# Decoder layer on one core: the output projection's weight scale, half by maximum on VectorE and half by row sums of squares on ScalarE

## What is computed

```
ctx = ctx.transpose(0, 2, 1, 3).reshape(N, S, N_HEADS * D_HEAD)
return ctx @ Wo + bo
...
x = x + _L0_attn_ref(_layernorm(x, axis=-1), Wq, Wk, Wv, Wo, bo)
```

## Time and profile before

| | us |
|---|---|
| median of 3 runs | 1280.59 |
| the three runs | 1277.7, 1280.98, 1280.59 |
| the profiled execution, whole time | 1277.78 |
| its span, first to last instruction | 1276.0 |
| PE busy | 1214.5 (95%) |
| DVE busy | 941.7 (74%) |
| ACT busy | 603.6 (47%) |
| POOL busy | 567.5 (44%) |
| mean granted TensorE clock | 0.989 |

### The profile page before, as it was taken

How to read it: one execution, slowest core, us unless ns; L and a number is a source line. 1 busy time by engine, 2 the same in 40 slices (tenths; PEclk the granted TensorE clock), 3 DMA queues, 4 the chain that set the end, 5 groups by cost and what they waited for, 6 DMA issues and landing times.

```text
span 1276.0 us, 20047 instructions
## 1 busy us (share of the span) xinstructions
PE 1214.5 (95%) x7263; PEld 828.6 (65%) x7278; DVE 941.7 (74%) x1283; ACT 603.6 (47%) x718; POOL 567.5 (44%) x491
## 2 busy tenths in 40 slices
PE   4977999999999999999999879999799999999998
PEld 3644555657557566575565457777587877877784
DVE  5799778877887788788887968888736545554654
ACT  5685584674765847747658610000134323432331
POOL 1444253543634535435355429999433222322321
PEclk9999999999999999999999989999899999999999
DMA  9462323542435235434355346775000000000000
GB/s 307 131 204 89 110 69 112 153 152 86 132 127 152 83 104 154 148 92 126 111 160 171 127 97 131 148 136 126 1 1 1 18 18 3 15 16 17 1 18 33
DMA packets 128006, 123.77 MB, mean 97 GB/s; under 512 B 31628, under 2 KB 89234, under 8 KB 127954
## 3 DMA queue, kind: packets, MB, share of 16 engines
q1 hardware_dynamic: 103000, 116.86, 30.5%
q10 hardware_dynamic: 24960, 6.29, 3.4%
HBM read 81.63 MB, written 35.21 MB: 92 GB/s over the span
## 4 chain that ended last, share of the span: by engine, by line
PE 80%; ACT 6%; DVE 6%; issue 5%; POOL 2%; DMA 1%; SPq 0%; ACTq 0%; DVEq 0%; POOLq 0%
PE bank L815 12%; PE bank L581 9%; PE bank L582 9%; PE bank L583 9%; PE bank L863 9%; PE bank L864 9%; PE bank L666 6%; PE bank L886 4%; PE bank L885 4%; PE bank L667 3%; PE bank L645 3%; PE bank L644 3%; ACT region_c L984 2%; POOL parts L1755 1%; ACT rsum L955 1%
## 5 line engine op out<-in xcount | busy, mean ns | idle before, releaser
L863 PE MATMUL bank<-h_hi,guT 128*128 128x256 f16 x1024 | 226.3, 274 | 1.4 <-DVE h_lo L1643 1.4
L864 PE MATMUL bank<-h_lo,guT 128*128 128x256 f16 x1024 | 226.2, 274 | 0.0
L1755 POOL TENSOR_TENSOR parts<-parts 128x512 f32<-128x512 f32 x80 | 130.6, 1636 | 180.8 <-DVE parts L1238 180.5
L581 PE MATMUL bank<-hT_hi,w_hi 128*128 128x256 f16 x640 | 175.9, 275 | 0.5 <-DVE hT_lo L1223 0.5
L582 PE MATMUL bank<-hT_lo,w_hi 128*128 128x256 f16 x640 | 175.8, 275 | 0.0
L583 PE MATMUL bank<-hT_hi,w_lo 128*128 128x256 f16 x640 | 175.7, 275 | 0.0
L815 PE MATMUL bank<-kv,toep 128*128 128x288 f32 x640 | 159.4, 413 | 5.4 <-POOL kv L1797 2.9
L1760 POOL TENSOR_SCALAR_AFFINE_SELECT region_c<-region_c 128x512 f32<-128x512 f32 x128 | 103.2, 830 | 120.8 <-ACT region_c L987 120.8
L815 PEld LDWEIGHTS bank<-kv,toep 128*128 128x128 f32 x640 | 123.4, 193 | 40.9 <-DVE prod L1606 3.3
L666 PE MATMUL bank<-region_c,v 128*128 128x512 f32 x256 | 133.3, 602 | 13.3 <-DVE ctx L1259 13.1
L984 ACT ACTIVATE region_c<-bank,cap_scale 128x1536 f32<-128x1536 f32 x64 | 98.7, 1542 | 52.8 <-PE bank L645 52.5
(11 more groups left out here) (161 smaller groups left out, 2512.6 us busy)
## 6 DMA issues: line engine op xcount, KB each, us to landing
unit_halves<-halves SPq DMA_DIRECT2D x80, 256.0 KB, 2.3
q_both<-unit_halves SPq DMA_DIRECT2D x64, 256.0 KB, 3.0
wffn<-w_gu SPq DMA_DIRECT2D x8, 1024.0 KB, 5.5
q_high<-unit_halves SPq DMA_DIRECT2D x64, 128.0 KB, 3.1
toep<-kernel_padded SPq DMA_DIRECT2D x32, 256.0 KB, 4.0
cpair<-ctx_pairs SPq DMA_DIRECT2D x32, 176.0 KB, 4.8
xin<-x SPq DMA_DIRECT2D x8, 512.0 KB, 3.5
region_o<-wq SPq DMA_DIRECT2D x4, 1024.0 KB, 12.1
```

What stands on the lines that cost most here:

```text
L581: pe.matmul(dst, lh, rh, start=first and k == 0, stop=False)
L863: pe.matmul(dst, guT[:, k, col:col + P], h3_hi[:, p, k, :], start=(k == 0), stop=False)
L864: mm = pe.matmul(dst, guT[:, k, col:col + P], h3_lo[:, p, k, :], start=False, stop=(k == DB - 1))
L1755: pool.tensor_tensor(slot[:, 0], slot[:, 0], slot[:, 1], ALU.add).then_inc(unit_summed, 1)
```

## The change

Wo's size is found in two ways. Pieces 0, 1, 3 and 5 still go by maximum on DVE, one at the end of each of the steps 4 to 7. Pieces 2, 4, 6 and 7 go by row sums of squares on ACT (`sum_wo_rows`, one in step 5, one in step 6, two in step 7); their by-product goes to `wo_hi[0]`. In step 8 DVE squares the four maxima, takes the larger of maxima and row sums, reduces over four and lays the diagonal (`largest_row_of_wo`). `find_scale` then takes the square root's exponent for weight 6 too, by the same number of steps.

SP issues four pieces (2 to 5) after unit 7's load back, and 6 and 7 after unit 8's. ACT's row sums of Q3 move behind the values' high part. PE's `top(I_O)` is written at step 9 ahead of `values`, which is the same place in PE's order. ACT's `high_wo(0)` and `(1)` move ahead of `high_unit(1, 2)`. `lay_bias(0)` waits for the key bias alone, and `bo` is waited for at the first `output`.

```
         BY_ROWS = range(I_K + 1, I_O)
+        WO_BY_MAX, WO_BY_ROWS = (0, 1, 3, 5), (2, 4, 6, 7)
...
-            sp.dma_start(key_bias_s[bias_rows], key_bias).then_inc(consts_in, 16)
+            sp.dma_start(key_bias_s[bias_rows], key_bias).then_inc(key_bias_in, 16)
...
-            sp.dma_start(bo_s[:], bo.partition_broadcast(P)).then_inc(consts_in, 16)
+            sp.dma_start(bo_s[:], bo.partition_broadcast(P)).then_inc(bo_in, 16)
...
-                if n == UNITS - 1:
+                if n == 8:
                     sp.wait_ge(w_rounded, 1)
-                for c in range(2 * (n - 6), 2 * (n - 5)) if n >= 6 else ():
+                for c in {6: (0, 1), 7: (2, 3, 4, 5), 8: (6, 7)}.get(n, ()):
                     sp.dma_start(wo_raw[c], wo.rearrange("(k p) n -> p k n", p=P)[:, o_rows[c], :]).then_inc(wo_in[c], 16)
...
+                    if step == NG + 1:
+                        pe.wait_ge(tanh_done, NG)
+                        top(I_O)
                     values(0, step - 2, True)
...
-                    if step == NG:
-                        pe.wait_ge(tanh_done, NG)
-                        top(I_O)
...
+            def sum_wo_rows(c):
+                act.wait_ge(wo_in[c], 16)
+                n = WO_BY_ROWS.index(c)
+                if n:
+                    act.wait_ge(wo_row_summed, n)
+                act.activation(wo_hi[0], wo_raw[c], ACT.Square, accum_out=wmax_row[:, n:n + 1]).then_inc(wo_row_summed, 1)
...
                 high_unit(0, 0, True)
-                sum_rows(I_Q[3])
                 high_unit(0, 1, True)
                 high_weight(I_V)
+                sum_rows(I_Q[3])
                 high_unit(0, 2, True)
...
+                    if step == NG + 1:
+                        for c in range(O_SHIFT):
+                            high_wo(c)
                     if 7 <= step < 7 + len(AHEAD_BANKS):
                         high_unit(1, step - 7)
...
-                    if step == NG + 1:
-                        for c in range(O_SHIFT):
-                            high_wo(c)
+                    for c in {5: (2,), 6: (4,), 7: (6, 7)}.get(step, ()):
+                        sum_wo_rows(c)
...
-                if n in BY_ROWS:
+                if n != I_K:
...
                 if c == 0:
-                    dve.wait_ge(consts_in, 16 * N_CONST)
+                    dve.wait_ge(key_bias_in, 16)
...
-                if c == O_PIECES - 1:
-                    dve.wait_ge(wpiece_done, O_PIECES)
-                    dve.tensor_reduce(wmax[:, I_O:I_O + 1], wmax_piece[:], AX_X, ALU.max).then_inc(wmax_done, 1)
-                    square(I_O)
+            def largest_row_of_wo():
+                dve.wait_ge(wpiece_done, len(WO_BY_MAX))
+                dve.tensor_tensor(wmax_piece[:], wmax_piece[:], wmax_piece[:], ALU.mult).then_inc(wpiece_done, 1)
+                dve.wait_ge(wo_row_summed, len(WO_BY_ROWS))
+                dve.wait_ge(wpiece_done, len(WO_BY_MAX) + 1)
+                dve.tensor_tensor(wmax_piece[:], wmax_piece[:], wmax_row[:], ALU.max).then_inc(wpiece_done, 1)
+                dve.wait_ge(wpiece_done, len(WO_BY_MAX) + 2)
+                dve.tensor_reduce(wmax[:, I_O:I_O + 1], wmax_piece[:], AX_X, ALU.max).then_inc(wmax_done, 1)
+                square(I_O)
...
+                    if step == NG:
+                        largest_row_of_wo()
                     normalise(0, step - 2, True)
...
-                    for c in {4: (0, 1), 5: (2, 3), 6: (4, 5), 7: (6, 7)}.get(step, ()):
+                    for c in {4: (0,), 5: (1,), 6: (3,), 7: (5,)}.get(step, ()):
                         largest_of_wo(c)
...
                     if n == EARLY - 1:
+                        dve.wait_ge(bo_in, 16)
                         for i in range(TT):
                             output(0, i)
```

More of the change, by code:

```diff
@@ L152, in decoder_layer @@
             wmax = sb1("wmax", [P, SCALES])
-            wmax_piece = sb1("wmax_piece", [P, O_PIECES])
+            wmax_piece = sb1("wmax_piece", [P, O_PIECES // 2])
+            wmax_row = sb1("wmax_row", [P, O_PIECES // 2])
             wtop = sb1("wtop", [P, SCALES])
@@ L245, in decoder_layer @@
         BY_ROWS = range(I_K + 1, I_O)
+        WO_BY_MAX, WO_BY_ROWS = (0, 1, 3, 5), (2, 4, 6, 7)
         def square_and_ones(n):
             return (early_squares[:, n], early_squares[:, SCALES]) if n != I_O else (wo_square, wo_ones)
-        consts_in = sem("consts_in")
+        key_bias_in = sem("key_bias_in")
+        bo_in = sem("bo_in")
         ident_in = sem("ident_in")
@@ L260, in decoder_layer @@
         wpiece_done = sem("wpiece_done")
+        wo_row_summed = sem("wo_row_summed")
         wmax_done = sem("wmax_done")
@@ L353, in decoder_layer @@
         out_stored = sem("out_stored")
-        N_ROPE, N_CONST = 2, 2
+        N_ROPE = 2
         QUANT_STORES = 16 * (1 + WQT - GUT)
@@ L1327, in largest_of_wo @@
             def largest_of_wo(c):
+                n = WO_BY_MAX.index(c)
                 dve.wait_ge(wo_in[c], 16)
-                dve.tensor_reduce(wmax_piece[:, c:c + 1], wo_raw[c], AX_XY, ALU.max, apply_absolute_value=True
+                dve.tensor_reduce(wmax_piece[:, n:n + 1], wo_raw[c], AX_XY, ALU.max, apply_absolute_value=True
                                   ).then_inc(wpiece_done, 1)
-                if c == O_PIECES - 1:
-                    dve.wait_ge(wpiece_done, O_PIECES)
-                    dve.tensor_reduce(wmax[:, I_O:I_O + 1], wmax_piece[:], AX_X, ALU.max).then_inc(wmax_done, 1)
-                    square(I_O)
+            def largest_row_of_wo():
[7 more added lines that the diff above has]
+                square(I_O)
             def low_wo(c):
```

## The result

The changed kernel takes 1284.53 us in the median of 22 runs (1280.32 to 1287.85), the kernel before 1280.28 in 22 runs beside it (1277.67 to 1282.93). The ratio is 1.0029, with a 95% interval of 1.0020 to 1.0038. That is 4.2 us slower, small but clear of the noise, and outside the forecast range, whose upper end was 1283.4. The profiled execution took 1282.67 us, its span 1280.9 against 1276.0.

What follows compares the result with a forecast made beforehand. DVE's path to low_wo(0), which output(0, 0) waits for, was taken to bound the kernel. A gain of 0.2 us there and 0.8 lost to the clock gave +0.6: 1278.4 in the profiled execution, 1281.2 on the median, range 1277.0 to 1283.4.

Steps and rivals of the forecast that it cites:

- What bounds it: First batch, steps 4 to 9: DVE's work sets low_wo(0), for which output(0, 0) waits; PE is busy from 120.48 on.
- Bias semaphore, row sums of Q3: Start of the kernel, rotate(0, 0) and first tanh: gain 0 from the semaphore, 0 to 0.04 us from the row sums.
- The reductions: DVE, maxima of Wo's pieces: four fewer at 1.17 us each, 4.7 us less work.
- ACT's Squares: ACT, steps 5 to 7: about 1.2 us each, covered by waits for scores and for normalise(5).
- The queue: SP: two more pieces ahead of unit 8's store delay its load back 2.8 us and scores(7) by 2.5.
- The two small operations: DVE, before normalise(6): two added instructions on four columns, 0.4 us together, between 0.3 and 0.6.
- The clock before output(0, 0): PE's pause of up to 4.7 us there: a clock fall costs 0 to 1.7 us, half taken, 0.8.
- The sum: normalise(5) 2.1 us late, then 6.94 to normalise(6); low_wo(0) gains 0.2, the clock costs 0.8: +0.6 us.
- B: Rival: lower clock after PE's longer pauses, at scores(7) and from output(0, 0) onward; +2.8 us, 1283.4; chance 0.14.
- C: Rival: SP's queue costs 3.2 us instead of 2.8, and some tenths again; 1281.6 to 1282.1; chance 0.16.
- A: Rival: unit 8's store is not held up by the pieces of Wo; gain 3.0 us, 1277.6; chance 0.24.

Runs made afterwards that it cites:

- e9: Kernel before with only the early edits: the bias row's own semaphore and ACT's row sums of Q3 behind the values' high part; 1280.43 us, ratio 1.0001.
- e2: Changed kernel with SP's old places for the pieces of Wo; 1281.56 us, ratio 1.0005.
- e7: e5 plus 12 unread matmuls in PE's pause before output(0, 0); 1278.41 us, ratio 0.9984 to the kernel before.
- e10: e8 without the unread matmuls; 1278.37 us, ratio 0.9983 to the kernel before.
- e12: Changed kernel with the two two-input operations on four columns moved into step 7, ahead of rotate(1, 1), form untouched; 1280.66 us, ratio 1.0006.
- e1: Changed kernel with the two-input operations on four columns replaced by one-input forms; 1283.2 us, ratio 1.0015.
- e5: Changed kernel with the edits of e1 and e2 together; 1279.07 us, ratio 0.9995 to the kernel before.
- e8: e7 with pieces 4 to 7 of Wo all behind unit 9's load back; 1275.99 us, ratio 0.9969 to the kernel before.
- e11: e8 with 20 unread matmuls in place of 12; 1276.62 us, ratio 0.9970 to the kernel before.
- e3: Changed kernel with 16 unread matmuls in PE's pause before output(0, 0); 1281.12 us, ratio 1.0004.
- e4: Kernel before with nothing but SP's new places for the pieces of Wo; 1282.04 us, ratio 1.0010.

## Why the prediction was wrong, point by point

**What bounds it.** Right: DVE's path to low_wo(0) decides output(0, 0), and from there on PE carries every difference to the mark (164.72 to 164.75 from output(0, 0) in the five traces without a low clock). From ctx of normalise(6) to low_wo(0) it was 8.13 us before and 121.40 - 113.27 = 8.13 after.

**Bias semaphore, row sums of Q3.** Right as far as e9 shows: no change, within 1.5 us either way.

**The reductions.** Right in size: one takes 1.22 for the 1.17 priced, and normalise(3) starts 20.34 after normalise(0) against 21.32.

**ACT's Squares.** Right: 1.06 and 0.20, partly side by side, 1.15 from start to end, and hidden: in e2, e7 and e10 normalise(4) still starts 0.7 earlier than before (27.27 to 27.29 against 27.97).

**The queue.** The size of the first delay was right, 2.67 for the 2.8 priced, in this trace; the others had 2.6 to 4.3. The step that failed is "what hangs on it reaches only normalise(4), some tenths later than before, and is swallowed ahead of scores(7)". It took scores(6) and the work behind them to be at full clock. scores(6) started 3.1 us late, and at half clock: their six matmuls took 1.2 more, and values(4) behind them kept take_sums(4) waiting 0.58 more. Of these nearly 5 us, ACT's and DVE's slack took up 2, and normalise(4) came 2.82 late.

e12 shows what the queue alone does to normalise(4). Its scores(6) start 23.04 after normalise(0), the changed kernel's 23.09, but at full clock (0.39 for the first, 0.61 there):

```profile
88.33 0.39 PE L648 MATMUL bank<-q_both,k_high 128*128 128x512 f16 x1 [1.21 <-DMA q_high<-unit_halves]
```

There normalise(4) starts at 28.92, not 30.79. So of the 2.82 the clock made 1.87 and the queue 0.95; against e2, which lacks both, the queue made 1.63. PE, in order, reached scores(7) 4.04 us late: 3.13 from the late start of scores(6), 2.48 more for the same work at the lower clock, less 1.57 of waits that the trace of before has on that way (1.09 and 0.48) and this one has not. So scores(7), and not unit 9's load back, set normalise(5), 3.77 late where 2.1 was predicted. At full clock PE would have reached them at 94.24, and unit 9's queries, issued at 91.36, landed 2.8 to 3.9 us later: an estimate from these rows is 1.6 to 2.6 us late, where the prediction had 2.5. In the other variant unit 9's load back is the gate: PE waits for it before scores(7) for 3.26 us in e1, 2.81 in e5 and 2.33 in e12, and for 1.16 and 1.02 in e7 and e2 with the old queue.

The wait for unit 8 did not cause that fall, which began ahead of it. All 14 traces have the pause that ends at 81.89 in the changed kernel (2.72 to 2.74 us); behind it the clock fell in six (changed, e1, e12, e8, e9, e11) and stayed up in eight. e9 has before's queue and all its reductions. In the other five of the six it was back at 1.00 by 88; in the changed kernel it stayed low through the wait for unit 8, to 93. In e3 and e4 the clock fell only at the end of that wait, of 3.08 and 3.90 us.

**The two small operations.** This step failed outright: priced at 0.4 together with bounds of 0.3 and 0.6, measured 2.23, by the row of a one-input reduction. The upper bound should have come from a two-input operation beside POOL. DVE's timeline of before has low_unit, with two inputs in SBUF, in both settings:

```profile
32.73 1.28 DVE L1386 TENSOR_TENSOR halves<-parts,halves 128x512 f16<-128x512 f32 x1 [0.61 <-ACT halves L968]
...
36.08 0.68 DVE L1386 TENSOR_TENSOR halves<-parts,halves 128x512 f16<-128x512 f32 x1
```

The first started while POOL was at its additions, which ran to 33.45; the second started 0.16 ahead of one (36.24). That is 0.6 more on 512 columns, from rows that were there to be read. normalise(5) to (6) was to take 6.94; it took 8.90, and 7.12 to 7.66 in the seven traces where the two don't stand under POOL's instructions (in e10, the 7.66, normalise(5) itself waits 0.34 for POOL's low_ctx).

**The clock before output(0, 0).** The pause was forecast at 4.7 and was 4.60, but the fall was given half its price, 0.8. It cost 2.27, 0.6 more than the 1.7 taken as the ceiling. That was read where PE worked 3.7 us at the lower level (111.71 to 115.39); here it was 4.6 (122.78 to 127.40). In the six traces with a pause of 3.85 or more before output(0, 0) the clock fell every time, so half a chance was too little; but at the time only pauses of up to 2.91 could be read.

**The sum.** On the profiled executions: -1.09 of the run's own lead, +3.77 at normalise(5), +0.25 to normalise(6), -0.64 to ctx behind it (the wait of 0.68 for POOL is gone), +2.27 by the clock: +4.56 at the mark, 4.9 at the end; 0.3 us are not accounted for. **The rivals.** B named the clock, with the wrong stretch for its first fall (scores(6) rather than (7)) and without the small operations, at 1283.4; C, a dearer queue, is what the other four traces with the new queue show, where unit 9's load back came 3.6 to 5.0 later. A is excluded: in none of the five did the store overtake the pieces.

## What to carry to other kernels

Before loads are issued earlier, look at what stands behind them in the same queue: with 1 MB more ahead of it, a small store on the path came back 2.6 to 4.3 us later here. Moving the large loads behind the store brought low_wo(0) 0.7 us earlier in e8 than in e7, and the reductions and Squares that they feed lost nothing by it. Price a tiny VectorE operation by its number of SBUF inputs and by what GpSimd runs at that moment, not by its columns alone, and look for a row of the same form in the same company: the diagonal, one tile and one scalar per partition, doubled beside POOL too. When work is taken off the engine that PE waits for, check the pauses that are left: the low clock behind a longer pause gave back 1.6 to 2.8 us of a gain. Unread matmuls kept it where they left 0.24 us of the pause or less (e3, e11), and not where they left 1.96 (e7, e8).

## What was not expected of the hardware

A product and a maximum on 128x4 values took 1.22 and 1.01 us instead of 0.16, because POOL was working. Before output(0, 0) the clock fell with pauses of PE of 1.96 and 3.19 us and did not with 2.91, 1.15, 0.24 and 0.23; with 3.85 to 4.60 it always fell. Behind one and the same pause of 2.7 us, earlier in the batch, it fell in six traces of fourteen: the same length of pause came with and without a fall. The same order of instructions had a unit's load back at 24.99, 25.16 and 26.97 us after the same mark in three traces (e2, e7, e5).
